# A Winograd form of the gate and up products in six of eight FFN blocks of a two-layer transformer kernel

## What is computed

```python
x = x + _L0_attn_a_ref(_layernorm(x, axis=-1), ...)
x = x + _L0_ffn_ref(_layernorm(x, axis=-1), L0_ffn_w_gate, L0_ffn_w_up, L0_ffn_w_down)
x = x + _L0_attn_b_ref(_layernorm(x, axis=-1), ...)
x = x + _L0_ffn_ref(_layernorm(x, axis=-1), L0_ffn_w_gate, L0_ffn_w_up, L0_ffn_w_down)

def _L0_ffn_ref(x, w_gate, w_up, w_down):
    gate = jnp.einsum('bsd,hd->bsh', x, w_gate)      # 512 -> 2048
    up = jnp.einsum('bsd,hd->bsh', x, w_up)
    gated = jax.nn.silu(gate) * up
    return jnp.einsum('bsh,dh->bsd', gated, w_down)  # 2048 -> 512
```

## Time and profile before

| | |
|---|---|
| median of 3 runs (lowest, highest) | 2179.28 us (2178.76, 2180.1) |
| the profiled execution | 2179.44 us |
| its span | 2177.7 us |
| PE busy | 2113.8 us, 97% of the span |
| DVE, POOL, ACT busy | 58%, 31%, 24% |
| granted TensorE clock, mean | 0.997 |

### The profile page before, as it was taken

How to read it: one execution, slowest core, us unless ns; L and a number is a source line. 1 busy time by engine, 2 the same in 40 slices (tenths; PEclk the granted TensorE clock), 3 DMA queues, 4 the chain that set the end, 5 groups by cost and what they waited for, 6 DMA issues and landing times.

```text
span 2177.7 us, 34223 instructions
## 1 busy us (share of the span) xinstructions
PE 2113.8 (97%) x11056; PEld 1486.4 (68%) x11056; DVE 1253.6 (58%) x2476; ACT 530.9 (24%) x1076; POOL 668.9 (31%) x508
## 2 busy tenths in 40 slices
PE   6999999999999999999989999999999999999998
PEld 5555478888755548888865554888877554588886
DVE  6766564544676647444467665644456767454445
ACT  1344420000144441000014454100011444310001
POOL 3324233332312323323231233333323223233322
PEclk9999999999999999999999999999999999999999
DMA  4333111111323211111242321111113232111113
GB/s 130 94 79 79 31 36 52 49 58 39 79 70 79 70 31 49 50 48 49 68 129 70 79 69 40 39 59 39 49 40 81 68 81 68 40 49 49 59 39 97
DMA packets 59748, 135.15 MB, mean 62 GB/s; under 512 B 10784, under 2 KB 11808, under 8 KB 59552
## 3 DMA queue, kind: packets, MB, share of 16 engines
q1 hardware_dynamic: 59552, 132.71, 21.6%
HBM read 77.62 MB, written 4.19 MB: 38 GB/s over the span
## 4 chain that ended last, share of the span: by engine, by line
PE 88%; issue 5%; DVE 2%; POOL 2%; ACT 1%; DMA 1%; SPq 0%; DVEq 0%; POOLq 0%; ACTq 0%
PE ring L898 13%; PE ring L899 13%; PE ring L900 13%; PE bank L1011 13%; PE ring L965 8%; PE bank L989 7%; PE bank L898 7%; PE bank L900 7%; PE bank L899 7%; PE ring L889 1%; ACT prob L560 1%; DMA area<-nm_lo 1%; POOL area L438 1%; DVE xn L699 1%; POOL prob L463 1%
## 5 line engine op out<-in xcount | busy, mean ns | idle before, releaser
L898 PE MATMUL ring<-xt_hi,area 128*128 128x512 f32 x1248 | 489.8, 392 | 1.1 <-DVE kq_parts L688 1.1
L899 PE MATMUL ring<-xt_lo,area 128*128 128x512 f32 x1248 | 486.4, 390 | 0.0
L900 PE MATMUL ring<-xt_hi,area 128*128 128x512 f32 x1248 | 486.0, 389 | 0.0
L699 DVE CUSTOM_DVE_ANT_0 xn<-ring,mask_row 128x128 bf16<-128x128 f32 (+7 forms) x512 | 374.5, 749 | 99.9 <-PE ring L965 93.9
L560 ACT ACTIVATE prob<-bank 128x512 f32<-128x512 f32 (+3 forms) x768 | 335.0, 489 | 342.4 <-PE bank L989 341.6
L436 POOL TENSOR_SCALAR area<-w_stage 128x1024 fp32r<-128x1024 f32 x131 | 144.4, 1103 | 762.2 <-PE bank L900 404.7
L766 DVE TENSOR_TENSOR prob<-prob,ring 128x512 f32<-128x512 f32 x128 | 87.8, 686 | 456.9 <-ACT prob L578 456.9
L438 POOL TENSOR_TENSOR area<-w_stage,area 128x1024 fp32r<-128x1024 f32 x131 | 322.8, 2464 | 10.9
L578 ACT ACTIVATE prob<-ring 128x512 f32<-128x512 f32 x128 | 76.5, 598 | 970.4 <-PE ring L900 970.4
L898 PEld LDWEIGHTS ring<-xt_hi,area 128*128 128x128 f32 x1248 | 234.3, 188 | 59.1 <-issue 9.8
L900 PEld LDWEIGHTS ring<-xt_hi,area 128*128 128x128 f32 x1248 | 234.3, 188 | 49.1
(11 more groups left out here) (78 smaller groups left out, 2053.4 us busy)
## 6 DMA issues: line engine op xcount, KB each, us to landing
w_stage<-ffn_w SPq DMA_DIRECT2D x96, 512.0 KB, 3.3
area<-kq_parts SPq DMA_DIRECT2D x336, 128.0 KB, 2.4
w_stage<-attn_w SPq DMA_DIRECT2D x35, 512.0 KB, 3.3
x<-x_in SPq DMA_DIRECT2D x24, 256.0 KB, 3.9
area<-attn SPq DMA_DIRECT2D x48, 128.0 KB, 2.3
out<-x SPq DMA_DIRECT2D x16, 256.0 KB, 2.2
bias_rows<-row_bias SPq DMA_DIRECT2D x10, 256.0 KB, 4.2
area<-nm_hi SPq DMA_DIRECT2D x32, 8.0 KB, 1.8
```

Source lines behind the costliest of these rows:

```text
L699: dve.tensor_tensor_reduce(out=sum_out[:, RING[name] % 2, 0:keys], in0=src[:, 0:keys], in1=mask_row[:, TOKENS - keys:], scale=1.0, scalar= ...
L898: pe.matmul(dst, ah, bh, start=first and k == 0, stop=False)
L899: pe.matmul(dst, ah, bl, start=False, stop=False)
L900: ins = pe.matmul(dst, al, bh, start=False, stop=last and k == n - 1)
```

## The change

In blocks 1 to 6 (`QUAD_FIRST` to `QUAD_LAST`) the gate product and the up product of a block (256 hidden rows, 512 inputs, 1024 tokens) are each seen as a product of two 2x2 block matrices: weights in quarters A11 to A22 (128 hidden rows by 256 inputs), tokens in quarters X11 to X22 (256 inputs by 512 tokens). They are made by Winograd's scheme, with seven block products m1 to m7 in place of eight. A block product is 6 matmuls; gate and up (w = 0, 1) make 14 products, 84 matmuls, where 96 were.

Four of the seven take sums of weight quarters. POOL makes them from the weights in `w_stage` (`quad_sums`, four instructions of 128x256) and splits them (`s_split`, two of 128x1024) ahead of its own slot's split. Four take differences of token quarters, made once per iteration: six sums on DVE (`diff_sum`, 128x1024), four copies to hi on ACT (`diff_to_hi`), four subtractions on DVE (`diff_to_lo`). For them ACT keeps an fp32 copy of the second half of the tokens (`xt_late`), made ahead of `xt_hi`.

PSUM holds three pairs of banks, x, y and z, whose roles rotate from block to block. m1, m6, m5 and m3 add up in x, with copies to SBUF by ACT in between (`keep`); m7 and m4 add up in y; m2 goes to z. DVE adds y or z onto the kept copies (`quad_add`), ACT takes silu in place, DVE multiplies (`quad_multiply`), ACT copies to hi (`quad_hi`) and DVE subtracts for lo (`quad_lo`). For the output pair (0, 1) the banks of x are used as they are. With six banks so taken, rows have only banks 2 and 3 in steps 1 to 11. The rows of the block before stand behind m7, m6, m5 and m2; in block 1 there is one row of step 1 behind each. Steps 14 and 15 are made as before, but with `down(12)` between the two halves of `gate_up(14, *)`. POOL also writes the ones rows of `k_stack` anew (2x6144), since sums lie there.

```diff
+PRODUCTS = ("m1", "m7", "m6", "m5", "m2", "m3", "m4")
+OUTPUTS = ((1, 1), (0, 0), (0, 1), (1, 0))
+DIFFS_BESIDE = ((), ((("sum", 4), ("lo", 1)), (("sum", 5), ("lo", 2))))
+DIFFS_FIRST = (("sum", 0), ("sum", 1), ("sum", 2), ("sum", 3), ("lo", 0))
+DIFF_HI_BESIDE = ((0, 1), (2,))
+ROWS_BEHIND = ("m7", "m6", "m5", "m2")
...
@@ POOL, split_weights @@
+                if part < 2 and QUAD_FIRST <= b <= QUAD_LAST:
+                    quad_sums(it, b, part, w_stage[:, j % 2, :])
+                    s_split(it, b, part)
...
@@ ACT @@
+                if name in (("ln2", 2), ("ln2", 3)):
...
+                    act.activation(late, src, ACT.Copy)
                 act.activation(dst, src, ACT.Copy).then_inc(xt_hi_ready, 1)
...
+                for s in range(1, QUAD_STEPS[0]):
+                    for t in range(BT):
+                        if s == QUAD_STEPS[0] - 1:
+                            for i in DIFF_HI_BESIDE[t]:
+                                diff_to_hi(i)
+                        silus(s, t)
+                diff_to_hi(3)
+                for b in range(QUAD_FIRST, QUAD_LAST + 1):
+                    for m in KEPT:
+                        for w in range(2):
+                            keep(b, m, w)
+                    for which in OUTPUTS:
+                        quad_silu(b, which)
+                        quad_hi(b, which)
...
@@ DVE @@
+                def quad_block(b):
+                    add_rows(2 * b - 1)
+                    quad_add(b, (1, 1), 0)
+                    quad_add(b, (1, 1), 1)
+                    if b > QUAD_FIRST:
+                        add_rows(2 * b - 2, range(2))
+                    quad_multiply(b, (1, 1))
+                    quad_add(b, (0, 0), 0)
+                    quad_add(b, (0, 0), 1)
+                    quad_lo(b, (1, 1))
+                    if b > QUAD_FIRST:
+                        add_rows(2 * b - 2, range(2, CT))
+                    quad_multiply(b, (0, 0))
+                    quad_lo(b, (0, 0))
+                    quad_multiply(b, (0, 1))
+                    quad_lo(b, (0, 1))
+                    quad_add(b, (1, 0), 0)
+                    quad_add(b, (1, 0), 1)
+                    quad_multiply(b, (1, 0))
+                    quad_lo(b, (1, 0))
...
@@ PE @@
+                    if m == "m1":
+                        pe.wait_ge(w_split, it * SLOTS + FFN_SLOT0 + 3 * b + w + 1)
...
+                    elif m == "m7":
+                        if b == QUAD_FIRST:
+                            pe.wait_ge(diff_ready, it * 4 + 1)
+                            pe.wait_ge(ring_drained, drained(it, ("gu", 2 * b - 1, 0)))
+                        else:
+                            pe.wait_ge(hidden_done, hidden_count(it, b - 1, (0, 1)))
...
+                    else:
+                        if b == QUAD_FIRST and m != "m3":
+                            pe.wait_ge(diff_ready, it * 4 + 3)
+                        pe.wait_ge(product_kept, kept_count(it, b, {"m6": "m1", "m5": "m6", "m3": "m5"}[m], w))
...
+                def quad_block(b):
+
+                    late = [(2 * b - 1, t) for t in range(CT)]
+                    rows = [late[0:2], late[2:4], [(2 * b - 2, 0), (2 * b - 2, 1)], [(2 * b - 2, 2), (2 * b - 2, 3)]]
+                    if b == QUAD_FIRST:
+                        rows = [[one] for one in late]
+                    for m in PRODUCTS:
+                        for w in range(2):
+                            product(b, m, w)
+                        if m in ROWS_BEHIND:
+                            for s, t in rows[ROWS_BEHIND.index(m)]:
+                                down_row(s, t)
```

More of the change, by code:

```diff
@@ L137, in ring_order @@
     yield from (("gu", 0, 0), ("gu", 0, 1), ("ln2", 2), ("ln2", 3))
-    yield from (("gu", s, t) for s in range(1, STEPS) for t in range(BT))
+    yield from (("gu", s, t) for s in range(1, STEPS) for t in range(BT) if s not in QUAD_STEPS)
 TAKE_AFTER = (8, 17)
@@ L424, in split_weights @@
                     after = last_product(before)
-                    if after[0] == "rows":
+                    if after[0] == "product":
+                        wait_alone(pool, product_full, products(it, *after[1:]))
+                    elif after[0] == "rows":
                         wait_alone(pool, rows_full, it * ROWS + after[1] + 1)
@@ L449, in last_product @@
                 x_last = b * CHUNKS + CHUNKS - 1
-                return ("rows", x_last * CT + CT - 1) if part == 2 else ("gu", x_last, BT - 1)
+                if part == 2:
+                    return "rows", max(row_at(b * CHUNKS + c, CT - 1) for c in range(CHUNKS))
+                return ("product", b, "m4", part) if QUAD_FIRST <= b <= QUAD_LAST else ("gu", x_last, BT - 1)
             def inverse_deviation(it, ln, c):
@@ L892, in iteration, with three @@
             def iteration(it):
[L893 removed]
+                def three(dst, terms, first=True, last=True, more=False):
                     n = len(terms)
                     for k, (ah, al, bh, bl) in enumerate(terms):
[L898 to L900 removed]
+                        pe.matmul(dst, ah, bh, start=first and k == 0, stop=False, skip_group_check=more)
+                        pe.matmul(dst, ah, bl, start=False, stop=False, skip_group_check=more)
+                        ins = pe.matmul(dst, al, bh, start=False, stop=last and k == n - 1, skip_group_check=more)
                     return ins
@@ L1166, in iteration @@
                         down(d)
+                for b in range(QUAD_FIRST, QUAD_LAST + 1):
+                    quad_block(b)
+                for t in range(BT):
+                    gate_up(STEPS - 2, t)
+                    down(STEPS - 4 + t)
+                down(STEPS - 2)
                 for t in range(BT):
```

282 lines of the change are left out of this document (247 added, 35 removed).

## The result

| | before | changed |
|---|---|---|
| median (lowest, highest; runs) | 2179.02 us (2176.01, 2180.1; 4) | 2207.72 us (2202.88, 2210.87; 4) |
| the profiled execution, its span | 2179.44, 2177.7 us | 2210.27, 2208.5 us |
| mean granted clock | 0.997 | 0.981 |

The changed kernel takes 1.013 times as long (95%: 1.0114 to 1.0147). 72 matmuls per iteration are gone, which should have given back 65.2 us; instead the kernel takes 28.7 us longer (medians). So 93.9 us were lost by medians, 96.0 by the two profiled executions, 24.0 per iteration.

What follows compares the result with a forecast made beforehand. PE was taken to bound the kernel, busy for 2113.8 of 2177.7 us. 2179.4 - 65.2 removed + 84 for waits and late copy + 5 for the clock = 2203 us; 8 in 10: 2133 to 2242.

Steps and rivals of the forecast that it cites:

- the likeliest case: Whole kernel: DVE's differences and POOL's sums and splits take turns; 2203 us, own range 2180 to 2230, chance 0.51.
- Removed work: FFN, 6 blocks and 4 iterations: 288 matmuls left out at 0.2263 us each save 65.2 us.
- Steady state: Blocks 3 to 6: no cost, 29.9 us per block, covered by 1.2 us at the narrowest place.
- the rival with a stalling steady state: Steady blocks: m6 waits for ACT's copy of m1, or POOL becomes the bound; 2223 or 2251 us, chance 0.17.
- Turns: DVE instructions with two SBUF operands and POOL's alternate; a 128x1024 difference ends 1.08 us behind POOL's end.
- the rival in which turns cost little: Whole kernel: only 0.7 us and up to 3 us at entry and exit stay; 2130 us, chance 0.12.
- Entry to block 1: Waits per iteration: m1's second half 1.3 us, m7 0.4, first row of step 1 6.8, m6 4.5.
- Block 2: Block 1 into 2: m7 waits 3.5 us and m6 0.8 us, 4.3 us per iteration.
- Exit: `down(12)` waits 3.0 us per iteration for DVE's product and subtraction of (1, 0) of block 6.
- Late copy: Block 0: ACT copies `ln2` 3 twice, so `gate_up(1, 0)` begins 0.7 us later per iteration.
- The clock: Entry: waits of 6.8 and 4.5 us may lower the granted clock; 1.2 us per iteration, between 0 and 3.6.
- waits of PE: PE's waits at the entry, ahead of block 2's m7 and m6, and at the exit; 81 us over four iterations.

Runs made afterwards that it cites:

- the last experiment: Changed kernel with start in block 2, differences early, rows of the first block two and two, down(12) behind gate_up(14, *): 2130.02 us, 0.977 of before.
- Experiments 1 and 2: Changed kernel with the differences' second operand in PSUM (1): 2158.77 us; changed kernel with POOL's sums and their splits cut to few columns (2): 2156.75 us.

## Why the prediction was right, and where it was not

The sign, the mechanism and the place of every long wait came out; 2203 us was forecast and 2207.72 measured, inside the likeliest case's own range. Point by point:

- **Removed work.** 65.2 us of matmuls, and that they are worth it where PE is busy: the last experiment accounts for it within 0.7 us.
- **Steady state.** Blocks 3 to 6 were to cost nothing at 29.9 us each. They last 29.92 us each and PE is never idle. POOL's quarter sums at 0.75 us (between 0.60 and 1.30) take 736 to 738 ns on the mean in the twelve splits that lie in the buffer of `xt_late`, and 833 to 1043 in the others, waits for DVE included. So the rival with a stalling steady state fell.
- **Turns.** Forecast 1.08 us behind POOL's end for a 128x1024 difference on DVE; 1.08 and 1.09 seen. Experiments 1 and 2 show the cause at the entry from either side. With the entry's turns gone the kernel is at 2157 to 2159 and not at the 2130 of the rival in which turns cost little, since block 2 and the exit still wait.
- **Entry to block 1.** m1's second half, m7, the first row and m6 were forecast at 13.6, 15.4, 25.0 and 30.9 us behind `gate_up(1, 0)`'s start. They begin at 14.7, 16.4, 24.1 and 29.4. Together 11.8 us late and not 13.0. m1's own wait was 2.2 and not 1.3 us, and m7 then had none. The idle time ahead of the first row is 3.4 to 5.0 us and ahead of m6 2.4, not 6.8 and 4.5, for the reason below.
- **Block 2.** 4.3 us forecast, 3.5 ahead of m7 and 0.8 ahead of m6. The waits were 3.15 ahead of m7, and 0.83 ahead of m6 in one iteration of four. In the second iteration the delay was 6.2 us in all, since part of the matmuls ahead ran slow.
- **Exit.** 3.0 forecast, 3.1 of wait. **Late copy.** 0.7 forecast, 0.68.
- **The clock** is the term that was mis-sized: 1.2 us per iteration was forecast, between 0 and 3.6, and 4.8 against before was measured, above the upper bound. I had expected a fall only behind the two long waits of the entry, and it came behind the waits of block 2 and `down(12)` too. The account of the 96.0 us, over four iterations:

| | forecast | measured |
|---|---|---|
| waits of PE | 81 | 62.6 |
| slow time, against before | 5 | 26.5 |
| (of it in the shadow of a wait) | - | 7.3 |
| late copy | 3 | 2.7 |
| sum | 89 | 91.8 |

62.6 is the five lines of PE's waits, of the first only the long ones, and the 0.8 us once ahead of m6 of block 2, for ACT's copy of m1. Slow time by place: 7.3 us ahead of m6 in the entry, 7.6 behind it, 7.1 behind block 2's wait, 6.3 behind `down(12)`'s, and 1.6 elsewhere, where before had 3.4. What lies ahead of m6 replaces idle time, since PE would have waited for DVE anyway: hence the shorter waits. What lies behind a wait comes on top: 21.0 us from the entry on, 5.3 per iteration, and not 1.2. The waits, with that shadow, were 11 us less than forecast, the clock 14 us more against before (19.2 for 5): two errors that nearly cancel, so that it is in part luck that 2203 came within 5 us of the measured time. 4.2 us of the 96.0 stay unassigned, 1.5 of them in a longer wait of the transposes for `xn`, outside the FFN.

## What to carry to other kernels

DVE's instructions with two SBUF operands and POOL's take turns here, so work added to both engines lasts as long as both together. It costs where both have a backlog at the same time, not on average: DVE and POOL were busy for 66% and 48% of this kernel. Look in the timeline for the stretch where one of the two is idle and put the other's two-operand work there, and give what stays in turn some cover. And a saving that holds in the steady state can be lost at entry and exit: 24.0 us per iteration went there against 16.3 saved, and giving up one of six blocks (10.9 us in all) made room to hide the entry.

## What the runs showed of the hardware beyond what was expected

- In one of four iterations the granted clock fell to the level of 1.2 GHz right behind a wait of 2.18 us (window 870 to 872), in the others only with the longer wait that follows; behind waits of 3.2 and 3.1 us it fell in three of four iterations each. With the entry filled, the second iteration showed falls behind the waits of block 2 and `down(12)`, where it had shown them in the FFN at the entry only. What decides which wait brings it wasn't settled.
- An fp32 operation of 128x1024 on DVE takes the same time from two SBUF operands (1218 to 1230 ns) as from one in PSUM (1213 to 1217), as long as POOL is out of the way.
